# A one-core transformer block: when the attention stage's DMA queue issues its large transfers relative to the small send of row maxima

## What is computed

```python
q, k, v = split(x @ Wq), split(x @ Wk), split(x @ Wv)      # 16 heads of 8 channels
scores_dot = einsum('bihd,bjhd->bhij', q, k) * scale
q_cos, q_sin = q_amp * cos(q_phi), q_amp * sin(q_phi)      # amp: normalised softplus; phi: pi * tanh(x @ Wqp)
k_cos, k_sin = k_amp * cos(k_phi), k_amp * sin(k_phi)
scores_phase = (einsum(q_cos, k_cos) + einsum(q_sin, k_sin)) * scale
scores = where(causal, scores_dot + lam * scores_phase, -inf)
out = einsum('bhij,bjhd->bihd', softmax(scores), v) @ Wo
```

## Time and profile before

| | us |
|---|---|
| median of 3 runs | 1214.71 (1214.58 to 1220.33) |
| the profiled execution's own time | 1213.49 |
| its span | 1211.7 |
| attention, steady part (halves) | about 597 to 985 of the span |
| PE busy over the span | 1076.6 (89%) |
| DVE, ACT, POOL busy | 912.0, 656.1, 269.1 |
| DMA queue of SP and what moved over the span | 127.54 MB of 129.06 MB |

### The profile page before, as it was taken

The page is one execution under the profiler, slowest core; times in us unless marked ns, Lnnn a source line. Parts: engine busy times, 40 slices in busy tenths (PEclk is TensorE's granted clock), DMA queues, the critical chain, the costliest instruction groups (busy, mean ns, idle before and its releaser), DMA issues. The chain is left out here.

```text
span 1211.7 us, 16306 instructions
## 1 busy us (share of the span) xinstructions
PE 1076.6 (89%) x5200; PEld 644.0 (53%) x5200; DVE 912.0 (75%) x1927; ACT 656.1 (54%) x1205; POOL 269.1 (22%) x300
## 2 busy tenths in 40 slices
PE   4888988976999999778888888989998979999998
PEld 1223333323666767534455555655656647667775
DVE  3878899994887777668786886778876728887776
ACT  2244344444555555479666675666755656555554
POOL 2445455651000000012132221222222220000000
PEclk9889798996999999979689999999999989999999
DMA  5000000000332332057887877878677202323320
GB/s 203 0 1 1 0 0 0 1 1 0 101 110 78 105 98 71 4 127 222 300 228 193 210 189 191 200 185 210 154 192 190 61 1 90 121 80 112 114 97 20
DMA packets 57487, 129.06 MB, mean 107 GB/s; under 512 B 9152, under 2 KB 11200, under 8 KB 56128
## 3 DMA queue, kind: packets, MB, share of 16 engines
q1 hardware_dynamic: 55360, 127.54, 37.6%
q10 hardware_dynamic: 2048, 0.53, 0.2%
HBM read 88.72 MB, written 36.70 MB: 104 GB/s over the span
## 5 line engine op out<-in xcount | busy, mean ns | idle before, releaser
L1529 DVE TENSOR_REDUCE attn_maxima<-attn_ps_p 128x1 f32<-128x512 f32 (+3 forms) x235 | 145.8, 637 | 58.0 <-PE attn_ps_p L1014 48.8
L1940 ACT ACTIVATE moe_hidden<-moe_ps_h 128x512 f32<-128x512 f32 x128 | 76.4, 597 | 147.0 <-PE moe_ps_y L1878 141.9
L1447 POOL TENSOR_SCALAR_AFFINE_SELECT attn_probs<-attn_probs 128x512 f32<-128x512 f32 x128 | 84.8, 697 | 278.9 <-ACT attn_probs L1258 278.9
L2064 DVE TENSOR_TENSOR moe_gated<-moe_ps_y,moe_gate_all 128x512 f32<-128x512 f32 x106 | 73.1, 690 | 72.3 <-issue 44.2
L1009 PE MATMUL attn_ps_p<-attn_stack 96*128 96x384 f32 (+3 forms) x341 | 116.3, 383 | 8.7 <-DVE attn_maxima L1529 8.6
L1057 PE MATMUL attn_ps_q<-attn_stack 128*128 128x128 f32 (+3 forms) x343 | 106.8, 375 | 16.1 <-DMA attn_stack<-attn_neg_max 13.7
L601 POOL TENSOR_TENSOR rwkv_rs<-rwkv_recept,rwkv_state 128x512 f32<-128x512 f32 x64 | 75.9, 1186 | 109.5 <-DVE rwkv_state L683 106.9
L1529 DVE TENSOR_REDUCE attn_maxima<-attn_ps_t 128x1 f32<-128x384 f32 (+3 forms) x117 | 74.4, 636 | 32.2 <-PE attn_ps_t L1014 28.6
L683 DVE TENSOR_TENSOR_SCAN rwkv_state<-rwkv_decay,rwkv_kv 128x512 f32<-128x512 f32 x64 | 92.4, 1444 | 3.2
L2095 DVE TENSOR_TENSOR moe_hidden_low<-moe_hidden,moe_hidden_high 128x512 fp32r<-128x512 f32 x128 | 87.6, 685 | 7.3 <-ACT moe_hidden_high L1941 7.2
L1082 PE MATMUL attn_ps_o<-attn_probs,attn_v_ones 128*32 128x512 f32 (+3 forms) x1024 | 82.1, 439 | 1.7 <-POOL attn_probs L1447 1.7
(11 more groups left out here) (272 smaller groups left out, 2593.7 us busy)
## 6 DMA issues: line engine op xcount, KB each, us to landing
moe_gate_all<-moe_gates SPq DMA_DIRECT2D x128, 256.0 KB, 4.9
attn_kept<-parts SPq DMA_DIRECT2D x32, 768.0 KB, 4.7
attn_stack<-attn_kept SPq DMA_DIRECT2D x128, 192.0 KB
attn_stack<-attn_kept SPq DMA_DIRECT2D x128, 96.0 KB
value<-attn_values SPq DMA_DIRECT2D x35, 256.0 KB, 4.6
attn_values<-attn_early SPq DMA_DIRECT2D x2, 1792.0 KB, 9.3
attn_values<-attn_probs SPq DMA_DIRECT2D x2, 1792.0 KB, 13.0
experts_in_w<-in_w SPq DMA_DIRECT2D x2, 1024.0 KB, 10.4
```

Of the source, the lines that this page charges most:

```text
L1447: nc.gpsimd.affine_select(out=tile, in_=tile, compare_op=ALU.is_ge, fill=0.0, base=0, pattern=[[0, 4], [1, P]], channel_multiplier=-1).the ...
L1529: nc.vector.tensor_reduce(maxima[:, u % 2, h:h + heads, t], tiles, AX_X, ALU.max).then_inc(g_free, 1)
L1940: fn(hidden[:, s, 0:T], ps_h[s][0][:], ACT.Gelu)
```

## The change

`sent` is replaced by `sending`, which waits not for the landing of a send but for the exponential of the piece behind the one at which ACT issues it (piece 5 or 15, so exp_done = slots + 2). Keeps and fetches now stand directly behind such a step and ahead of the refill, where before one keep or fetch could stand ahead of the step or behind the refill. The seven fetched pieces are split 2, 3, 2 over three steps instead of 3, 4 over two.

```diff
--- before.py
+++ after.py
@@ -853,13 +853,15 @@
                 sp.wait_ge(v_copied, TURN_OF[b] + 1)
                 sp.dma_start(value_kept[b], home(b).rearrange("p n t -> p (n t)")).then_inc(stored[b], 16)
 
+            FETCHED = [range(0, 2), range(2, 5), range(5, 7)]
+
             def fetch(b, part):
                 if part == 0:
                     sp.wait_ge(stored[b], 16)
                     for s in range(2):
                         sp.wait_ge(low_ready[s], 3 * (b - 1))
                     sp.wait_ge(v_ready, b - 1)
-                for n in (range(0, 3) if part == 0 else range(3, 7)):
+                for n in FETCHED[part]:
                     at = slice(n * T, (n + 1) * T)
                     sp.dma_start(value_flat[b % 2][:, at], value_kept[b][:, at]).then_inc(loaded[b % 2], 16)
 
@@ -872,8 +874,9 @@
                 sp.dma_start(scratch[b][s].rearrange("n d h t -> (d h) n t")[:, at, :],
                              parts[s][:, at, :].bitcast(F32)).then_inc(kept[s], 16)
 
-            def sent(u, half):
-                sp.wait_ge(neg_max_landed[half], (u + 1) * 32)
+            def sending(u, half):
+                slots = u * PIECES + 4 if half else (u - 1) * PIECES + 14
+                sp.wait_ge(exp_done, slots + 2)
 
             def stack_heads(b, q, half):
 
@@ -919,27 +922,28 @@
             keep(1, 0, 1)
             keep(1, 1, 0)
             for b in range(LAST):
+                sending(2 * b, 1)
                 keep(b + 1, 1, 1)
-                sent(2 * b, 1)
-                refill(b, 0, 0)
                 if b + 3 < NB:
                     fetch(b + 3, 0)
+                refill(b, 0, 0)
                 if b == LAST - 1:
                     for s in range(2):
                         sp.wait_ge(low_ready[s], 3 * NB)
                     sp.wait_ge(v_ready, NB)
                     again.load(sp, *expert_sources)
-                sent(2 * b + 1, 0)
+                sending(2 * b + 1, 0)
                 if b + 3 < NB:
                     fetch(b + 3, 1)
                 refill(b, 0, 1)
+                sending(2 * b + 1, 1)
                 if b + 2 < NB:
-                    keep(b + 2, 0, 0)
-                sent(2 * b + 1, 1)
-                if b + 2 < NB:
-                    keep(b + 2, 0, 1)
+                    for part in range(2):
+                        keep(b + 2, 0, part)
+                if b + 3 < NB:
+                    fetch(b + 3, 2)
                 refill(b, 1, 0)
-                sent(2 * b + 2, 0)
+                sending(2 * b + 2, 0)
                 if b + 2 < NB:
                     keep(b + 2, 1, 0)
                 refill(b, 1, 1)
```

## The result

The changed kernel is slower: median 1228.45 us (1227.51 to 1230.83, 4 runs) against 1214.64 us (1213.68 to 1220.33, 4 runs), ratio 1.0116, 95% interval 1.0083 to 1.0148. The forecast was 1213.9 us, the range 1205 to 1222, and a change under 0.5% the likeliest case.

What follows compares the result with a forecast made beforehand. PE was taken to set the attention stage's pace, with DMA engines near enough to full to hold it up. - 16.3 + 12.6 + 2.4 + 0.5 = - 0.8 us gave 1213.9 us, range 1205 to 1222.

Steps and rivals of the forecast that it cites:

- the clock: PE's half-clock spells behind waits in the attention stage: counted as nothing, with 3 us either way.
- The waits that go: PE's waits for sends at the first piece of a half: 16.3 of 19.5 us removed.
- The refill behind v_ready: refill(b, 0, 0), b = 1 to 4, issued behind fetches waiting for v_ready: PE waits 12.6 us more, ends 0 and 18.6.
- ACT's wait for the last pieces: ACT's first use of fetched pieces in five batches, last fetch a step later: 0.5 us, ends 0 and 4.
- The sends behind two keeps: Send of the next unit's first half, behind two keeps, two fetches and a refill, five batches: 2.4 us, ends 0 and 6.
- Rival (1): At PE's score matmuls for b = 1 to 4 the refill is not awaited: 1201 to 1208 us, chance 0.20.
- Rival (4): SP's bursts stay in place, a refill being held by h_done: 1214.7 us; chance 0.58 together with the forecast.
- Rival (2): At the first piece of each half, what is issued behind a send holds it up: 1235 us, chance 0.09.
- the turns between queues: DMA engines alternate between queues by packet, so issue order gives nothing, the refill's 12.6 us stands alone: 1226; under Rival (2).
- Rival (3): All costs in the attention stage near their upper ends: + 7 us, 1219 to 1224 us, chance 0.13.
- The signs: Right: no send wait over 2 us (b = 0 to 5), four refill waits of 2.4 to 3.3; wrong: ACT waiting over 1.

Runs made afterwards that it cites:

- gate alone: Kernel before with only SP's step behind a send changed to wait for the next exponential, order and fetch split kept; ratio 0.9867, median 1201.01 us.
- refill first: Changed kernel with refill(b, 0, 0) put back ahead of the two fetches; ratio 0.9935 to the kernel before, median 1209.03 us.
- values early: Changed kernel with POOL's place_values(b + 1) ahead of its selects, SP's list untouched; ratio 0.9887 to the kernel before, median 1205.69 us.
- two parts late: Changed kernel with the fetch in two parts (2 and 5 pieces), the first still ahead of the refill; ratio 1.0061 to the kernel before, median 1223.78 us.
- two parts: The refill first kernel with the fetch in two parts (2 and 5 pieces) instead of three; ratio 0.9872 to the kernel before, median 1200.09 us.
- late fetch only: Kernel before with only the first part of the fetch (three pieces) moved ahead of refill(b, 0, 0); ratio 1.0148, median 1233.69 us.
- keep later: Changed kernel with refill ahead of fetches, POOL's copy ahead of its selects, and one keep moved behind the next send; ratio 0.9853, median 1199.2 us.
- load later: The keep later kernel with the expert weights' load moved behind the step that watches the next send; ratio 0.9835 to the kernel before, median 1195.7 us.

## Why the prediction was wrong, step by step

The measured time lies 14.5 us above the forecast and outside of its range. The step that failed is the clock, put at nothing; two smaller terms were mis-sized. By PE's waits for sends and refills alone the stretch would have lost 3.6 us (17.8 to 21.4), still inside of the range.

- **The waits that go: right in kind.** I put them at 16.3 us, with 2.4 left over for sends. The gate alone took 14.1 us of them in the stretch (17.8 to 3.7). In the changed kernel 10.4 are gone (17.8 to 7.4), where 13.9 was forecast.
- **The refill behind v_ready: right in place, cause and nearly in size.** Four waits at L1022, b = 1 to 4, 12.6 us forecast, 14.0 measured, inside of 0 to 18.6. From the first fetch to PE's matmul it is 10.6 to 11.2 us where 10.0 was taken; the 9.1 us in it held 0.4 for the landing behind the last packets (944.9 to 953.6) for which there was no row. Two experiments that make v_ready harmless (refill first, values early) remove the waits, and one that adds only the fetches' place to the kernel before brings them.
- **The clock: the step that failed.** "I count nothing, with 3 us either way" took the half-clock spells as even on both sides. Over whole executions the granted clock is 0.923 to 0.930 in the four runs of the changed kernel, 0.926 on average, and 0.935 on average in the 59 of the kernel before. As an estimate from these, the time times what the clock lacks to 1 is 91 us after and 79 before: up to 12 us of TensorE time lost to the clock, if PE were busy throughout, beside 3.6 us of waits. Filling the wait with useless work brings the clock back to 0.936 and gives 7 us of time; the gate alone has 0.942, and no spells where the kernel before had 14 to 34 us of them. So the fetches' place costs more than its waits: 22 to 23 us by two pairs of runs (changed and refill first, two parts late and two parts), and 18 us by a third (late fetch only and before). PE's waits for sends and refills grow by some 15, 12.8 and 13.6 us in these pairs, so 1.3 to 1.8 us of time for each us of waits.
- **ACT's wait for the last pieces: the second size that was off.** The step saw it, and took 0.5 us with 0 to 4. ACT waits 3.8 us in the changed kernel, up to 6.1 in its relatives. The two score buffers of lead did not cover it: a send stands right behind the wait, and PE waits 1.15 and 1.06 us for exponentials at 700.02 and 864.25, about 5 us behind ACT's waits. The two-parts version puts its price at some 8 us, two parts late at 7.
- **The sends behind two keeps: mis-sized, too, and by another cause.** 2.4 us were taken; in the stretch 7.4 are left, 1.5 of them for the load, so 5.9, near the upper end of 6. But 3.9 of these are the waits at 757.98 and 812.50, which go when the fetch has two parts and both keeps stay. They hang on the fetch's third part, either as 0.5 MB in front of the send or by ACT's wait ahead of it; the runs do not tell the two apart.
- **The sum.** By ratios: the gate - 1.3% (- 16 us), the fetches' place + 1.8 to 1.9% (+ 22), the third part + 0.6% (+ 8): + 14 us, and + 14 measured. Forecast were - 16.3, + 12.6, and 2.4 + 0.5 for what the third part brings. That the sum closes so well is in part luck, as each price is known to some 4 to 6 us either way.
- **Rivals.** Rival (1) falls: PE waits for the refill in all four places. Rival (4) falls too: the keeps and fetches did move, and the waits with them. Rival (2), traffic behind a send holding it up, falls with the gate alone, which runs 16 us faster with that traffic there. By the turns between queues that the Trainium skill ("DMA: Bandwidth & Descriptors", section "Queues, rings and completion order") describes, the prediction had 1226 us, near the 1228.45 measured. This is luck: there were to be hardly any waits for sends to gain, and the gate alone gains 14.1 us of them. Rival (3) named the right costs, but without the clock.
- **The signs.** Of those named beforehand, one for being wrong came: ACT waits up to 1.5 us at its first use of fetched pieces. Of those for being right, "no wait for a send over 2 us" failed once (2.22 us), and three of the four refill waits are over the 3.3 us named.

What stays open: which short pause of PE gets a half-clock spell, and how much of the 7.0 us of clock between the two first profiles is the change's, since the second profile of the kernel before has as much half clock as the changed one. That the change lowers the clock does not rest on these profiles but on the clocks of the runs, though the changed kernel itself has only four.

## What to carry to other kernels

A queue that is worked off in order makes every wait in it a wait of all that stands behind: before a small item is put ahead of a large one, look what the small one waits for (here POOL's copy, which by the prediction's rows comes 5 us later than the refill could go). Price PE's idle time at more than its length where the profile shows half-clock spells at it (here 1.3 to 1.8 times), and look at the granted clock of many runs, or at least at a second profile of the same program, before counting them. When a change bundles several edits, run each by itself: here one line was worth 1.3%, and its companions cost 2.5%.

## What the runs showed that was not expected

- The granted clock differs between two executions of one program with nearly the same sum of waits: 13.7 and 34.1 us of half clock in a stretch of 370 us, 332.0 and 340.6 us of PE busy.
- In the fourteen profiles there are 15 pauses of PE of 2.56 us and more in that stretch after its first 12 us. A half-clock spell stands at every one, beginning between 2.5 us ahead of its end and 1.8 us behind; at shorter pauses it stands in some places and not in others.
- In the three versions whose waits for sends sum to under 4 us and that have no other long wait (gate only, keep later, load later), there is no half clock in that stretch after its first 12 us, and the 2472 matmuls take 325.8 to 326.4 us.
- 48 matmuls of no use made a program some 7 us faster.
